# A mixture-of-experts stage rewritten as one program: router a sequence ahead, routed weights loaded in pieces, scratch cleared beside another stage

## The chip, the cores and the metric

The kernel runs on one core of a Trainium2 chip. The metric is the time of one execution on the device, in microseconds (us). The core has five engines that run their own instruction streams and meet at semaphores: TensorE (PE, matrix products), VectorE (DVE), ScalarE (ACT), GpSimd (POOL) and SyncE (SP, which here only starts transfers), and 16 DMA engines that move data between the chip's memory (HBM) and the core's own memory (SBUF). PE writes its results into banks of a small memory, PSUM, which DVE and ACT read.

## What is computed

16 sequences of 512 tokens with 256 features pass through six layers, each on the layer norm of x and with a residual sum. The two that the change is about are these (cut):

```python
def _L1_ffn_ref(x, router_w, router_b, routed_w1, routed_w3, routed_w2, shared_w1, shared_w3, shared_w2):
    logits = xf @ router_w + router_b                      # 8 experts
    topk_vals, topk_idx = jax.lax.top_k(logits, 2)
    sparse = sparse.at[jnp.arange(T)[:, None], topk_idx].set(topk_vals)
    gates = jax.nn.softmax(sparse, axis=-1)
    routed = jax.vmap(_expert, in_axes=(None, 0, 0, 0))(xf, routed_w1, routed_w3, routed_w2)
    routed_out = jnp.einsum('etd,te->td', routed, gates)
    shared_out = jax.vmap(_expert, in_axes=(None, 0, 0, 0))(xf, shared_w1, shared_w3, shared_w2).sum(axis=0)
    return (routed_out + shared_out).reshape(B, S, D)

def _expert(xf, w1, w3, w2):                    # hidden width 128
    return jax.nn.silu(xf @ w1) * (xf @ w3) @ w2

x = x + 0.5 * ffn(layernorm(x))
x = x + gated_linear_attention(layernorm(x))
x = x + 0.5 * ffn(layernorm(x))
x = x + 0.5 * moe(layernorm(x))        # moe0
x = x + attention(layernorm(x))        # 16 heads, softmax, a band of 0.1 near the diagonal
x = x + 0.5 * moe(layernorm(x))        # moe1, the same weights
```

## The kernel before

x (8192 tokens by 256 features, fp32) stays in SBUF for the whole kernel. The program is a row of stages with a barrier over all engines between them: constants, ffn0, `gla` (gated linear attention), ffn1, moe0, `att`, moe1. Within a stage each engine has a program written out by hand, in the order of the Python loops, and semaphores carry the dependences; no planner reorders anything. To keep fp32 precision every product is made of three PE products of parts: the high part of each operand (a rounded copy, usually made by ACT), and the low part (operand minus high, usually by DVE).

**The gated linear attention** (`gla_stage`) goes through the 16 sequences one by one. Per sequence a recurrence is solved by merging blocks in levels: PE makes 64 small products (L2201), DVE merges them (`merge`, L2514) and scales q (`raise_q`, L2530), POOL scales k (`raise_k`, L2453), and the next level's products wait for both. The DVE program also holds, for the sequence before, `o_norm` (reciprocal, then 4 instructions over 128x256, L2492) ahead of the level-1 merge, and the layer norm of the next sequence (4 instructions, L121).

**A MoE stage** (`moe_stage`) is five blocks one after another, each with a barrier behind it.

1. `prepare` loads the weights in 10 parts by SP (router, and w1, w3, w2 of experts 0 to 3, 4 to 7 and the two shared ones), makes the high parts on ACT (L637) and the low ones on DVE (L651). Attention uses the same helper with 4 parts. `whole_numbers` then makes tables of integers on POOL.
2. `dispatch_phase` goes through the 16 sequences. For sequence b DVE normalises the rows (L966), PE transposes them (L817), ACT copies the high part (L894) and DVE the low one (L972). PE computes the hidden layer of the first shared expert, with the router's products strewn between (`hidden`, L843, router L824 and L827), then the second expert, the transposes of b+1, the output (L858) and `places` (L868, L871, L873), which count the tokens ahead of each token per expert. DVE takes the logits (L994, L996), chooses the two best (`choose`, L1002 to L1021, ending with the margin that the gates come from), ACT makes the sigmoid of the margin (L914; sigmoid and silu need different tables of ACT, so a table load stands before each change), DVE writes gate and destination beside the row (L1027 to L1034) and the row index (L1039 to L1045). ACT makes the second copy of the rows (L900). POOL then issues 8 indirect DMAs (L946) that scatter the rows, 1040 bytes each, into an HBM scratch `expert_rows` by expert; a ring of 3 row buffers is freed by `sent`. `places` writes into the PSUM bank of the second shared expert, so it waits for that expert's silu.
3. `table_phase` computes on DVE, from the counts, which expert and which rows each of 39 tiles of 512 rows takes (L1110 to L1130).
4. `expert_phase`: ACT first issues 8 DMAs of 520 KB that zero the rows behind each expert's last (L1234), SP loads the tiles, and PE, ACT, DVE and POOL compute them and scatter the results.
5. `combine_phase` adds the two results of each token to x.

The lines of the dispatch loop of PE that matter, as written:

```python
for b in range(B):
    hidden(b, 0)
    if b:
        output(b - 1, 1)
    hidden(b, 1)
    if b + 1 < B:
        transpose(b + 1)
    output(b, 0)
    places(b)
```

## Time and profile before

| | us |
|---|---|
| time, median of 3 runs | 3865.52 |
| the runs | 3856.92, 3866.49, 3865.52 |
| the profiled execution, its time | 3864.73 |
| its span | 3862.7 |
| moe0: weights prepared | 1344.3 to 1361.2 |
| moe0: dispatch, first transposes to last row index | 1365.1 to 1605.6 |
| moe0: from there to the first tile's transposes | 1605.6 to 1636.8 |
| moe0: tiles | 1636.8 to 1913 |
| moe1: dispatch, the same bounds | 3238.8 to 3478.7 |
| gated linear attention | 408 to 1003 |

The span counts from the profiled execution's first instruction to its last; the time has 2 us around it. In the views below a time stamp is us from the span's start. A row of the timeline gives start, duration, engine, line, operation, output and input, how many like instructions are drawn together, and in square brackets how long the engine stood idle before it and who released it. In a row of a stretch, (x12) is how many instructions started there, PEclk is the clock that TensorE was granted as a share of the full one, and DMA the busy share of the 16 DMA engines.

### The profile page before, as it was taken

To read this page: it belongs to the slowest core of one execution; us is meant where nothing else is said; L and a number is where in the kernel's file an instruction comes from. 1 tells how busy PE (TensorE), PEld (TensorE's weight loads), DVE (VectorE), ACT (ScalarE), POOL (GpSimd) and SP (SyncE) were. 2 spreads that over 40 slices of the span, in tenths; PEclk is the share of its full clock that TensorE was granted. 3 is DMA by queue.
4 is the path that set the end of the run, shared out by engine and by line. 5 is a ranking of instruction groups with operands and counts; after the bars stand their busy time and mean duration, and the time that the engine had idled before them with its cause. 6 is when DMAs were issued, how large, how long until landed. Compare 5 with 4: busy or idle time off the path is not lost. (4 is left out here: it accounts for less than half of the span.)

```text
span 3862.7 us, 72003 instructions
## 1 busy us (share of the span) xinstructions
PE 3120.2 (81%) x24192; PEld 2382.7 (62%) x24192; DVE 2530.4 (66%) x5327; ACT 1824.5 (47%) x3241; POOL 1631.9 (42%) x1347
## 2 busy tenths in 40 slices
PE   5999688888799889688507999999999996995880
PEld 4888577777688778576404555555555554884660
DVE  5666577877566678555375777777777765774552
ACT  2444244444355445255303666666666664543550
POOL 1665222222366545456552333333333332553665
PEclk9999899999899989799857999999999997987995
DMA  3000000000000022355443324324233221224547
GB/s 110 0 0 0 16 0 0 0 0 0 1 0 0 19 77 74 105 161 158 149 143 101 93 70 114 82 78 111 74 88 100 74 66 64 77 74 156 158 151 281
DMA packets 204552, 292.07 MB, mean 76 GB/s; under 512 B 21472, under 2 KB 136560, under 8 KB 204416
## 3 DMA queue, kind: packets, MB, share of 16 engines
q1 hardware_dynamic: 149760, 189.51, 17.8%
q0 software_dynamic: 27264, 75.01, 5.1%
q10 hardware_dynamic: 27392, 25.83, 2.0%
q8 instruction: 74, 1.21, 0.1%
q14 instruction: 62, 0.51, 0.0%
HBM read 146.47 MB, written 143.28 MB: 75 GB/s over the span
## 5 line engine op out<-in xcount | busy, mean ns | idle before, releaser
L1945 DVE TENSOR_REDUCE neg_max_sb<-s_ps 128x1 f32<-128x512 f32 x1024 | 692.4, 687 | 292.4 <-PE s_ps L1672 271.6
L1835 ACT ACTIVATE prob_sb<-s_ps 128x512 f32<-128x512 f32 x1024 | 602.5, 600 | 393.6 <-PE s_ps L1684 384.3
L1592 POOL TENSOR_TENSOR prob_sb<-prob_sb,band_sb 128x520 f32<-128x520 f32 (+1 forms) x256 | 285.2, 1114 | 715.5 <-ACT prob_sb L1835 715.3
L529 POOL TENSOR_TENSOR f_sq_lo_sb<-f_sq_sb,f_sq_hi_sb 128x512 fp32r<-128x512 f32 x256 | 329.5, 1295 | 348.4 <-ACT f_sq_hi_sb L504 348.4
L1684 PE MATMUL s_ps<-q_stack_sb,k_stack_sb 128*128 128x512 f32 x1024 | 450.9, 441 | 8.0 <-ACT prob_sb L1835 7.5
L1672 PE MATMUL s_ps<-k_stack_sb,q_stack_sb 96*128 96x512 f32 x1024 | 425.9, 419 | 33.6 <-DMA k_stack_sb<-qk_scratch 23.3
L1280 POOL DMA_INDIRECT ranked_rows<-m_y_gated_sb,slot_dest_sb x312 | 328.0, 1051 | 263.5 <-ACT m_y_gated_sb L1261 177.5
L946 POOL DMA_INDIRECT expert_rows<-rows_sb,row_index_sb x256 | 258.0, 1008 | 245.3 <-DVE row_index_sb L1045 173.6
L1684 PEld LDWEIGHTS s_ps<-q_stack_sb,k_stack_sb 128*128 128x128 f32 x1024 | 193.2, 189 | 256.7 <-ACT prob_sb L1835 131.3
L499 ACT ACTIVATE f_relu_sb<-ffn_hp_ps 128x512 f32<-128x512 f32 x256 | 153.4, 599 | 314.6 <-PE ffn_hp_ps L452 314.0
L1705 PE MATMUL pv_ps<-prob_sb,v_ones_sb 128*32 128x512 f32 x2048 | 273.2, 606 | 0.9 <-POOL prob_sb L1592 0.9
L566 DVE TENSOR_TENSOR f_sq_sb<-ffn_hp_ps,f_relu_sb 128x512 f32<-128x512 f32 x256 | 174.6, 686 | 134.4 <-ACT f_relu_sb L499 99.4
L464 PE MATMUL ffn_y_ps<-w_proj_tern_sb,f_sq_lo_sb 128*128 128x256 f32 x1024 | 256.2, 283 | 0.0
L1672 PEld LDWEIGHTS s_ps<-k_stack_sb,q_stack_sb 96*128 96x128 f32 x1024 | 196.8, 192 | 96.0 <-DVE neg_max_sb L1945 50.3
L464 PE MATMUL ffn_y_ps<-w_proj_tern_sb,f_sq_hi_sb 128*128 128x256 f32 x1024 | 255.3, 282 | 0.7 <-POOL f_sq_lo_sb L529 0.7
L1196 PE MATMUL moe_b_h_ps<-xnT_hi_sb,tile_weights_sb 128*128 128x512 f32 x624 | 214.4, 425 | 43.9 <-issue 23.6
L1292 DVE TENSOR_TENSOR xnT_lo_sb<-moe_b_tp_ps,xnT_hi_sb 128x1024 fp32r<-128x1024 f32 x78 | 95.5, 1224 | 222.5 <-issue 112.4
L843 PE MATMUL moe_a_h_ps<-xnT_hi_sb,w_sb 128*128 128x512 f32 x512 | 212.2, 482 | 29.1 <-DVE xnT_lo_sb L972 24.7
L452 PE MATMUL ffn_hp_ps<-xnT_hi_sb,w_fc_hi_sb 128*128 128x512 f32 x512 | 210.6, 411 | 21.0 <-DVE xnT_lo_sb L158 19.8
L452 PE MATMUL ffn_hp_ps<-xnT_hi_sb,w_fc_lo_sb 128*128 128x512 f32 x512 | 203.8, 398 | 0.0
L464 PEld LDWEIGHTS ffn_y_ps<-w_proj_tern_sb,f_sq_hi_sb 128*128 128x128 f32 x1024 | 194.4, 190 | 11.9 <-POOL f_sq_lo_sb L529 1.1
L452 PE MATMUL ffn_hp_ps<-xnT_lo_sb,w_fc_hi_sb 128*128 128x512 f32 x512 | 201.7, 394 | 0.0
(346 smaller groups left out, 7936.9 us busy)
## 6 DMA issues: line engine op xcount, KB each, us to landing
expert_in_sb<-expert_rows SPq DMA_DIRECT2D x78, 520.0 KB
qk_scratch<-qk_hi_sb SPq DMA_DIRECT2D x128, 256.0 KB
q_stack_sb<-qk_scratch SPq DMA_DIRECT2D x128, 192.0 KB, 4.0
k_stack_sb<-qk_scratch SPq DMA_DIRECT2D x128, 192.0 KB, 4.2
token_results_sb<-ranked_rows SPq DMA_DIRECT2D x32, 512.0 KB, 6.3
token_results_sb<-ranked_rows ACTq DMA_DIRECT2D x32, 512.0 KB, 6.0
qk_scratch<-qk_lo_sb SPq DMA_DIRECT2D x64, 256.0 KB
expert_rows<-zero_rows_sb ACTq DMA_DIRECT2D x16, 520.0 KB, 5.6
```

What stands on the lines that cost most here:

```text
L452: op = nc.tensor.matmul(hp[j % 2][:, :], a[:, k, j * P:(j + 1) * P], x[:, k, :], start=(k == 0 and i == 0), stop=(k == KT - 1 and i == 2))
L464: op = nc.tensor.matmul(y[:, t, :], r[:, j, t * P:(t + 1) * P], w.proj[:, j, :], start=(j == 0 and t % 2 == 0 and i == 0), stop=(j == JT - ...
L529: nc.gpsimd.tensor_tensor(sql[:, j, :], sq[:, j % 2, :], as_f32(sqh[:, j, :]), ALU.subtract).then_inc(low_ready, 1)
L946: nc.gpsimd.indirect_dma_start(scratch.rows, bass.IndirectOffsetOnAxis(ap=idx[:, b % RB, r, t:t + 1], axis=0), rows[:, b % RB, r, t, :], N ...
L1196: op = nc.tensor.matmul(o[i % 2][:, :], wt[:, i % 2, part, k, :], x[:, k, :], start=(k == 0 and n == 0), stop=(k == KT - 1 and n == 2))
L1280: nc.gpsimd.indirect_dma_start(scratch.ranked, bass.IndirectOffsetOnAxis(ap=dst[:, i % META, t:t + 1], axis=0), ys[:, i % 2, t, :], None). ...
L1592: nc.gpsimd.tensor_tensor(pr, pr, bcast(band[:, off:off + hi - lo].unsqueeze(1), [P, GH, hi - lo]), ALU.mult).then_inc(band_done, 1)
L1672: nc.tensor.matmul(s1p[n % 2][:, :], qs[r, g // 2, u, qt * P:(qt + 1) * P], ks[r, g // 2, j, :], start=True, stop=True).then_inc(s1_ready, 1)
L1684: nc.tensor.matmul(s2p[i % 2][:, :], ks[:, g // 2, j, kt * P:(kt + 1) * P], qs[:, g // 2, u, :], start=True, stop=True).then_inc(s2_ready, 1)
L1705: op = nc.tensor.matmul(pvp[2 * HD * i:2 * HD * (i + 1), :], vaug[:, kt, GH * g + i, :], prob[:, kt % 2, i, :], start=(kt == 0), stop=(kt ...
L1835: nc.scalar.activation(prob[:, kt % 2, i, :], s2p[i % 2][:, :], ACT.Exp).then_inc(exp_done, 1)
L1945: nc.vector.tensor_reduce(nm[:, g % 2, 2 * (i % 2) + i // 2, qt:qt + 1], s1p[n % 2][:, :], AXIS_X, ALU.max, negate=True).then_inc(max_done, 1)
```

## The change

**The offset.** `prepare` computes once per stage, for all tokens, minus mean times rstd (`core.offset`, one more wait and one DVE instruction of 128x64). With it a normalisation is one ACT instruction, scale and bias by pointer.

**In the gated linear attention** the layer norm of the next sequence and `o_norm` move from DVE to ACT; DVE keeps two short instructions (`o_factors`). SP clears the whole scratch `expert_rows` (70144 rows of 1040 bytes, 72.9 MB) with 4 DMAs in this stage, from a zero tile, and the stage's end waits for them.

**In the MoE stages** `prepare` takes only the router and the shared experts (4 parts). The routed weights come in 12 pieces (two experts and one of w1, w3, w2 each, 128x512) inside the dispatch loop, in sequences 0 to 11: SP loads into a ring of 2, ACT copies the high part, POOL subtracts the low one. Dispatch, table and tiles are now one block. In the loop the layer norm of the rows moves from DVE to ACT, the second copy of the rows from ACT to POOL, and the router becomes 16 products by themselves, one sequence ahead of the shared experts. `places(b)` uses the same bank as before and so now waits for the silu of sequence b-1's second expert. The tails behind the experts' last rows are zeroed in their 4 payload columns alone (16 bytes a row), and SP waits for all 8 of these DMAs before the first tile. The tiles' own loops and the combining phase are computed as before.

The core of the diff, in the dispatch loop. TensorE:

```diff
-            for b in range(B):
-                hidden(b, 0)
-                if b:
-                    output(b - 1, 1)
-                hidden(b, 1)
-                if b + 1 < B:
-                    transpose(b + 1)
-                output(b, 0)
-                places(b)
-            output(B - 1, 1)
+                    for b in range(B + 1):
+                        if b < B:
+                            router(b)
+                        if b:
+                            hidden(b - 1, 0)
+                        if b >= 2:
+                            output(b - 2, 1)
+                        if b + 1 < B:
+                            transpose(b + 1)
+                        if b:
+                            hidden(b - 1, 1)
+                        if b < B:
+                            places(b)
...
+                        if b:
+                            output(b - 1, 0)
+                    output(B - 1, 1)
```

In `places`:

```diff
-                pe.wait_ge(silu_ready, 2 * b + 2)
+                        if b:
+                            pe.wait_ge(silu_ready, 2 * b)
```

ScalarE:

```diff
-            x_high(0)
-            second(0)
-            for b in range(B):
-                silu_of(b, 0)
-                high_of(b, 0)
-                silu_of(b, 1)
-                if b + 1 < B:
-                    x_high(b + 1)
-                share_of(b)
-                high_of(b, 1)
-                if b + 1 < B:
-                    second(b + 1)
+                    normalise(0)
+                    x_high(0)
+                    normalise(1)
+                    for b in range(B + 1):
+                        if b:
+                            silu_of(b - 1, 0)
+                            high_of(b - 1, 0)
+                        if b < B:
+                            share_of(b)
+                        if b + 1 < B:
+                            x_high(b + 1)
+                        if b < len(routed):
+                            weight_high(b)
+                        if b:
+                            silu_of(b - 1, 1)
+                        if b + 2 < B:
+                            normalise(b + 2)
+                        if b:
+                            high_of(b - 1, 1)
+                        if b == B - 1:
+                            act.wait_ge(table_ready, 1)
+                            for e in range(EXPERTS):
+                                row = act.value_load(tail[0:1, e:e + 1], min_val=0, max_val=EXPERTS * REGION - TOKENS)
+                                nc.scalar.dma_start(scratch.rows[bass.ds(row, TOKENS), DM:ROW]
+                                                    .rearrange("(t p) d -> p t d", p=P), zero[:, :, :]).then_inc(tail_zeroed, 16)
```

GpSimd:

```diff
+                    second(0)
+                    for b in range(B):
+                        if b < len(routed):
+                            weight_low(b)
+                        if b + 1 < B:
+                            second(b + 1)
+                        pool.wait_ge(second_ready, b + 1)
+                        pool.wait_ge(payload_ready, b + 1)
+                        pool.wait_ge(index_ready, b + 1)
```

VectorE:

```diff
+                    for b in range(B + 1):
+                        if b < B:
+                            take_logits(b)
+                            choose(b)
+                        if b:
+                            product(b - 1, 0)
+                            low_of(b - 1, 0)
+                        if b >= 2:
+                            update(b - 2)
+                        if b < B:
+                            payload(b)
+                        if b + 1 < B:
+                            x_low(b + 1)
+                        if b < B:
+                            index(b)
+                        if b == B - 1:
+                            table()
+                        if b:
+                            product(b - 1, 1)
+                            low_of(b - 1, 1)
```

SyncE, ahead of the first tile:

```diff
+                    sp.wait_ge(table_ready, 1)
+                    for i in range(RB):
+                        sp.wait_ge(sent[i], PER_SENT * ((B - 1 - i) // RB + 1))
+                    sp.wait_ge(tail_zeroed, 16 * EXPERTS)
```

In the gated linear attention, on ScalarE, VectorE and SyncE in turn:

```diff
+                def o_norm(b):
+                    act.wait_ge(o_off, b + 1)
+                    for t in range(NC):
+                        op = nc.scalar.activation(og[:, t, :], og[:, t, :], ACT.Identity, bias=off[:, t:t + 1],
+                                                  scale=ors[:, t:t + 1])
+                    op.then_inc(on_ready, 1)
...
                     merge(b, 0)
                     if before:
-                        o_norm(b - 1)
+                        o_factors(b - 1)
                     merge(b, 1)
...
                     raise_q(b, 4)
-                    if more:
-                        norm.normalise(dve, b + 1)
                     merge(b, 5)
...
+                for i in range(CLEAR):
+                    part = slice(left * i // CLEAR, left * (i + 1) // CLEAR)
+                    sp.dma_start(cleared[:, part, :], bcast(zeros[:, :].unsqueeze(1), [P, part.stop - part.start, TILES * ROW])
+                                 ).then_inc(clear_done[i], 16)
```

ACT's instructions in the dispatch loop, one sequence's turn from a silu on, before (m_silu_sb is the silu, m_act_hi_sb the high part of the hidden layer, xnT_hi_sb that of the transposed rows):

```order
L904 ACTIVATE m_silu_sb<-moe_a_h_ps 128x512
L894 CAST xnT_hi_sb<-moe_a_tp_ps 128x1024
L914 ACT_TABLE_LOAD
L914 ACTIVATE share_sb<-margin_sb 128x32
L910 CAST m_act_hi_sb<-m_act_sb 128x512
L900 COPY rows_sb<-rows_sb 128x4x256
L904 ACT_TABLE_LOAD
L904 ACTIVATE m_silu_sb<-moe_a_h_ps 128x512
```

and with the change, in the same loop of ACT (xn_sb is where the silu now goes, w_sb a routed weight's high part):

```order
L1008 ACTIVATE xn_sb<-moe_h_ps 128x512
L1014 CAST m_act_hi_sb<-m_act_sb 128x512
L1018 ACT_TABLE_LOAD
L1018 ACTIVATE share_sb<-margin_sb 128x32
L1004 CAST xnT_hi_sb<-moe_tp_ps 128x1024
L1023 CAST w_sb<-routed_values_sb 128x512
L1008 ACT_TABLE_LOAD
L1008 ACTIVATE xn_sb<-moe_h_ps 128x512
L996 ACTIVATE rows_sb<-x_resident_sb,ln_minus_mean_rstd_sb,ln_rstd_sb 128x256 x4
```

Both silus of a sequence stood between two sigmoids with no table load between them; now the sigmoid of the next sequence stands between them, and the second silu, for which `places` waits, comes behind the sigmoid, the transposed rows' copy, the weight's copy and a table load.

PE's instructions around `places` before, with the next sequence's hidden layer and router behind it:

```order
L858 MATMUL moe_a_y_ps<-w2h_sb,m_act_lo_sb 128x256
L868 MATMUL moe_a_h_ps<-chosen_sb,below_sb 128x32
L871 MATMUL moe_a_h_ps<-chosen_sb,ones_sb 128x24
L871 MATMUL moe_a_h_ps<-chosen_sb,ones_sb 128x16
L871 MATMUL moe_a_h_ps<-chosen_sb,ones_sb 128x8
L873 MATMUL moe_a_h_ps<-seen_sb,ones_sb 128x32
L843 MATMUL moe_a_h_ps<-xnT_hi_sb,w_sb 128x512
L827 MATMUL moe_a_tp_ps<-router_w_hi_lo_sb,xnT_hi_sb 128x16
L843 MATMUL moe_a_h_ps<-xnT_hi_sb,w_sb 128x512
L824 MATMUL moe_a_tp_ps<-router_w_hi_lo_sb,xnT_lo_sb 128x8
```

and with the change, around `places` on PE:

```order
L883 MATMUL moe_h_ps<-xnT_hi_sb,w_sb 128x512 x2
L883 MATMUL moe_h_ps<-xnT_lo_sb,w_sb 128x512
L904 MATMUL moe_h_ps<-chosen_sb,below_sb 128x32
L907 MATMUL moe_h_ps<-chosen_sb,ones_sb 128x24
L907 MATMUL moe_h_ps<-chosen_sb,ones_sb 128x16
L907 MATMUL moe_h_ps<-chosen_sb,ones_sb 128x8
L909 MATMUL moe_h_ps<-seen_sb,ones_sb 128x32
L893 MATMUL moe_y_ps<-w2h_sb,m_act_hi_sb 128x256
```

`places` now stands directly behind the second expert's hidden layer (L883), whose silu it waits for, and an output (12 products, L893) stands behind it. Behind that output come the router's products of the next sequence, 16 of them without anything between, and then the hidden layer:

```order
L871 MATMUL moe_tp_ps<-router_w_hi_lo_sb,tile_weights_sb 128x8
L869 MATMUL moe_tp_ps<-router_w_hi_lo_sb,xnT_hi_sb 128x16
L871 MATMUL moe_tp_ps<-router_w_hi_lo_sb,tile_weights_sb 128x8
L883 MATMUL moe_h_ps<-xnT_hi_sb,w_sb 128x512 x2
L883 MATMUL moe_h_ps<-xnT_lo_sb,w_sb 128x512
```

(tile_weights_sb serves there as the third buffer of the transposed rows' low part.) Before, these 16 stood one or two at a time behind the twelve products of L843.

## Rows read from the trace of the kernel before

**Rows 1.** The page, part 1: busy us, share of the span, instructions of each engine

```profile
PE 3120.2 (81%) x24192; PEld 2382.7 (62%) x24192; DVE 2530.4 (66%) x5327; ACT 1824.5 (47%) x3241; POOL 1631.9 (42%) x1347
```

**Rows 2.** Stretches: gated linear attention, then moe0's weights, dispatch, dispatch to tiles

```profile
core 0: us, PE busy (x) PEld busy (x) DVE busy (x) ACT busy (x) POOL busy (x), PEclk, DMA share, GB/s
408.00:1003.00 595.00, 474.18 (x9344) 413.73 (x9344) 444.20 (x925) 235.64 (x388) 135.98 (x114) 0.97 0.00 1
1344.30:1361.20 16.90, 0.00 (x0) 0.00 (x0) 9.88 (x11) 8.50 (x11) 0.03 (x1) 0.50 0.76 234
1365.10:1605.60 240.50, 223.41 (x1306) 200.12 (x1307) 176.79 (x552) 115.13 (x144) 120.98 (x120) 0.88 0.19 69
1605.60:1636.80 31.20, 2.09 (x11) 1.73 (x9) 6.43 (x23) 0.00 (x0) 7.77 (x8) 0.50 0.39 128
```

**Rows 3.** The same view: moe1's dispatch

```profile
3238.80:3478.70 239.90, 223.35 (x1306) 200.16 (x1307) 176.35 (x551) 115.12 (x144) 121.48 (x120) 0.88 0.20 69
```

**Rows 4.** Timeline of one sequence in the gated linear attention, DVE, POOL and PE

```profile
645.54 2.58 DVE L2492 TENSOR_SCALAR g_og_sb<-g_og_sb,g_mv_sb,g_rstd_sb 128x256 f32<-128x256 f32 x4
646.36 1.61 POOL L2453 TENSOR_TENSOR g_ks_sb<-g_ks_sb,g_f_sb 128x512 f32<-128x512 f32 x1 [15.81 <-PE g_h_ps L2201]
649.18 0.53 PE L2201 MATMUL g_h_ps<-g_qp_sb,g_ks_sb 128*32 128x32 f32 x37 [1.41 <-DVE g_qp_sb L2530]
...
657.66 1.37 DVE L121 TENSOR_SCALAR xn_sb<-x_resident_sb,ln_mean_var_sb,ln_rstd_sb 128x256 f32 x4
```

**Rows 5.** The view by stretches: attention's weights, 4 parts

```profile
1995.90:2003.50 7.60, 0.00 (x0) 0.00 (x0) 3.29 (x5) 4.11 (x6) 0.02 (x1) 0.50 0.48 139
```

**Rows 6.** The same view: two sequences of moe0's dispatch, one after the other

```profile
1420.80:1434.00 13.20, 12.38 (x83) 11.15 (x82) 11.17 (x36) 7.20 (x9) 7.96 (x9) 1.00 0.23 81
1434.00:1451.90 17.90, 17.07 (x83) 15.31 (x82) 11.32 (x36) 7.19 (x9) 11.51 (x12) 0.71 0.24 87
```

**Rows 7.** Timeline of moe0's dispatch, PE from one output to the next

```profile
1479.59 0.36 PE L858 MATMUL moe_a_y_ps<-w2h_sb,m_act_hi_sb 128*128 128x256 f32 x1
...
1481.09 0.32 PE L868 MATMUL moe_a_h_ps<-chosen_sb,below_sb 128*128 128x32 f32 x2
...
1483.12 0.50 PE L843 MATMUL moe_a_h_ps<-xnT_hi_sb,w_sb 128*128 128x512 f32 x1 [0.82 <-DVE xnT_lo_sb L972]
...
1487.69 0.36 PE L858 MATMUL moe_a_y_ps<-w2h_sb,m_act_hi_sb 128*128 128x256 f32 x1
```

**Rows 8.** Timeline of the same stretch, DVE: choose, then a product

```profile
1478.58 0.42 DVE L1002 TENSOR_TENSOR above_sb<-logits_sb 128x256 f32<-128x256 f32 x1
...
1481.74 0.19 DVE L1021 SCALAR_TENSOR_TENSOR margin_sb<-logits_sb,both_sb 128x32 f32<-128x32 f32 x1
...
1482.98 0.68 DVE L978 TENSOR_TENSOR m_act_sb<-moe_a_h_ps,m_silu_sb 128x512 f32<-128x512 f32 x1
```

**Rows 9.** Timeline of the same stretch, ACT

```profile
1479.87 1.01 ACT L894 CAST xnT_hi_sb<-moe_a_tp_ps 128x1024 fp32r<-128x1024 f32 x1 [1.67 <-PE moe_a_tp_ps L817]
1480.91 1.28 ACT L914 ACT_TABLE_LOAD   x1
1482.20 0.23 ACT L914 ACTIVATE share_sb<-margin_sb 128x32 f32<-128x32 f32 x1
1483.70 0.62 ACT L910 CAST m_act_hi_sb<-m_act_sb 128x512 fp32r<-128x512 f32 x1 [1.27 <-issue]
...
1486.58 0.60 ACT L904 ACTIVATE m_silu_sb<-moe_a_h_ps 128x512 f32<-128x512 f32 x1
```

**Rows 10.** Groups by line: busy us, mean ns of one | idle time before them

```profile
L946 POOL DMA_INDIRECT expert_rows<-rows_sb,row_index_sb x256 | 258.0, 1008 | 245.3 <-DVE row_index_sb L1045 173.6 <-issue 71.7
```

**Rows 11.** Timeline from moe0's dispatch to its tiles, DVE, ACT's queue, PE

```profile
1620.92 0.17 DVE L1110 COPY count_sb<-moe_t_ps_ps 128x8 f32<-128x8 f32 x1 [12.34 <-PE moe_t_ps_ps L1098]
...
1626.80 12.62 ACTq L1234 DMA_DIRECT2D expert_rows<-zero_rows_sb  x8
...
1636.80 1.12 PE L1189 MATMUL moe_b_tp_ps<-identity_sb,expert_in_sb 128*128 128x128 f32 x4 [15.92 <-DMA expert_in_sb<-expert_rows]
```

1067 lines of the change are left out of this document (517 added, 550 removed).

## The prediction

> **What bounds the kernel now.** The page's first part comes first: PE is busy 81% of the span, DVE 66%, ACT 47%, POOL 42% [rows 1]. That is an average over unlike stages, so the view by stretches comes next, cut at the places that the change touches [rows 2]. In the gated linear attention (595 us) PE is busy 474 and DVE 444, and the DMA engines do nothing. While moe0's weights are prepared PE does nothing for 16.9 us; the transfers run at 234 GB/s and DVE and ACT work only as parts arrive. In the dispatch PE is busy 223 of 240.5 us, at a mean clock of 0.88. Between the last row index and the first tile lie 31.2 us in which PE does nearly nothing. moe1's dispatch is the same within 0.6 us [rows 3], so every term of a MoE stage counts twice.
>
> So in the dispatch PE is the bound, and what matters there is the clock. Two sequences, one after the other, with the same instructions take 13.2 us at clock 1.00 and 17.9 us at 0.71 [rows 6]: a fall to 1.2 GHz costs 4.7 us. 0.71 over 17.9 us is 10.4 us at half speed. A mean of 0.88 over 240.5 us [rows 2] is 58 us at half speed; some 16 of these are its start (the stretch before it stands at 0.50, and PE keeps that until large products have run), and the other 42 are four falls of 10.4. PE's rows show what they follow: an output, then places, 10 small products in 1.21 us (1481.09 to 1482.30), and a wait of 0.82 us for the low part of the next rows [rows 7]. That is 2.0 us without a large product, in every sequence; four of 16 such stretches end in a fall.
>
> **The change, part by part.** The sum is made against the profiled execution, 3864.7 us, which lies 0.8 under the median of the three runs.
>
> *Gated linear attention.* o_norm holds DVE for 2.58 us from 645.54. Only then can DVE merge level 1 and scale q, and PE waits 1.41 us for it, until 649.18; POOL's k is ready at 647.97 (646.36 + 1.61) [rows 4]. Without o_norm POOL ends last: PE starts some 0.95 us sooner. The layer norm (1.37 us of DVE [rows 4]) goes too, in a place where DVE is not always last; I take 0.3 of it. With 15 such sequences that is 15 x 1.25, about -18. Bounds: 15 x (1.41 + 0.5) = -29, and +5 if ACT, which gets 8 instructions of under 0.60 each (that is what 512 columns take [rows 9]), hands its next copy over late; ACT is busy only 236 of 595 us [rows 2]. The clearing of 72.9 MB takes 312 us at the 234 GB/s of the weight loads, under 595 us in which nothing else uses DMA [rows 2]: nothing. Should it not fit, only the end of the stage would wait, by the time over 595.
>
> *Prepare.* Attention's four parts are ready in 7.6 us [rows 5]; the MoE stage's ten take 16.9 [rows 2]. Four parts here too: -9.3 each. The extra DVE instruction hides under the loads.
>
> *Dispatch, start.* At half speed the transposes take 1.6 and the router's products 3.6; with the high part 1.0, the low part 1.2, logits and choose 3.8, places 1.8 and index 1.0 that is 14 us from the first transposes to the first index (an estimate from the prices below).
>
> *Dispatch, per sequence.* By work PE would need the 12.4 us that it is busy now [rows 6]. But places(b) now waits for silu(b-1,1), and that stands at the end of a chain that begins with the router's last product: two short additions 0.4 (like the 0.19 of L1021), choose 3.35 (1478.58 to 1481.93), product 0.68 [rows 8], high part 0.62, table load 1.28, sigmoid 0.23, copy of the rows' high part 1.01, the weight's high part 0.62 (same shape as L910), table load 1.28, silu 0.60 [rows 9]: 10.1, with hand-overs 10.2 us. ACT's table loads come in its stream behind the instruction ahead, and a load does not wait for its sigmoid's input (1480.91, before the margin at 1481.93 [rows 8, 9]); but the load stands behind the high part, which waits for the product, so nothing hides it now. In these 10.2 us PE has two hidden layers, one output and the transposes: 12 products of 512 columns at 2.4 GHz are 2.56 us, 2.8 with their starts, one output is 1.5 (1479.59 to 1481.09 [rows 7]), and the transposes are what is left of the 12.4 after hidden and router, hidden, two outputs and places: 12.4 - 4.57 - 2.8 - 3.0 - 1.2 = 0.8. So 2 x 2.8 + 1.5 + 0.8 = 7.9. PE then stands idle for some 2.3 us ahead of places in every sequence. Behind the silu follow places 1.2, output 1.45 and the router's 16 products: hidden and router together take 4.57 (1483.12 to 1487.69 [rows 7]), so 1.8. Period: 10.2 + 1.2 + 1.45 + 1.8 = 14.65 us, and 14.05 in the three last, which have no weight to copy. The layer norm on ACT (4 instructions) lies behind the silu and so beside places, output and router. At full clock: 14 + 12 x 14.65 + 3 x 14.05 = 232 us, against 240.5: -8.5.
>
> The Trainium skill, "ScalarE: Activation LUTs" (What ACT_TABLE_LOAD costs), puts a change of table at about 2.66 us, with a drain behind the load. The row shows 1.29 from the start of the load to its sigmoid; by the page's figure a sequence would be 2.8 us longer and the kernel some 80 us slower, and the trace speaks against it.
>
> *Dispatch, clock.* Now the stretch without a large product is 2.3 + 1.2 = 3.5 us, then 1.45 us of output, then 1.8 us of router products of 16 and 8 columns: 6.75 us with one output in it, where before there were 2.0. A longer sparse stretch cannot make fewer falls than now unless it is its idle part alone that counts, so I take a fall in every second sequence, 8 of 16, at 4.7 each: 38 us. Bounds: none and 15. The dispatch takes 270, +29.5 each.
>
> *POOL.* 8 indirect DMAs take 10.3: 1.01 each, and 0.3 of issue ahead of each but the first (71.7 us over 224 [rows 10]). The weight's low part is 128x512 with two inputs, 1.61 [rows 4]; the second copy, 128x1024, costs between nothing and twice that. At 2.0, POOL needs 13.9 a sequence, under 14.65: nothing. At 3.2 it would be 15.1 and bind by 0.5.
>
> *Gap to the tiles.* Now: index, 8 indirect DMAs, barrier, table from 1620.92, then ACT issues 8 tail DMAs in 12.62 us from 1626.80, and a tile's rows come at 1636.80 [rows 11]. With the change the table (5 us with its count) starts behind the index and beside POOL; one product and one high part later, at about 6.5, ACT starts to issue: 6.5 + 12.6 = 19. SP waits for all eight, then loads: from the first tail's issue to the transposes are 10.0 us today, less its own issue of 1.6, so 8.4 for a landing and a load, and 8 to 9.5 with the last one's short runs. Transposes at 27 to 28.5, against 31.2 now: -2.7 each, between -6 (a landing of 16-byte runs is quick) and +3 (if such runs take 6 us more than full rows). The shared experts of the last sequence (two hidden layers, two outputs) fill part of it. Tiles and combining are untouched: nothing.
>
> Sum: -18 + 2 x (-9.3 + 29.5 - 2.7) = -18 + 35 = +17: 3881.7, say **3882 us**. A measurement of this kernel can tell about 0.3%, 12 us, from no change.
>
> **The rivals.**
>
> *The falls stay at four or so in a dispatch* (3 to 5), because they depend on how the sequences' period meets the chip's, not on the stretch's length. For: only 4 of 16 equal stretches fell. Then 4 x 4.7 = 19, dispatch 251, +10.5 each: -18 + 2 x (-9.3 + 10.5 - 2.7) = -21, 3844 us.
>
> *No falls, faster.* PE never stands idle for long: 2.3 us at a stretch. Then dispatch is 232: -18 + 2 x (-9.3 - 8.5 - 2.7) = -59, 3806 us. Against it: falls came after waits of 0.82 us [rows 7]. The Trainium skill, "TensorE: Matmul & The Clock Gate" (Why this matters for your kernels), warns of idle gaps of PE between bursts longer than these; by that rule nothing here would fall, and by it nothing should have fallen before either, which the clock of 0.71 contradicts.
>
> *A fall in every sequence, slower still.* 15 x 4.7 = 70, dispatch 302: -18 + 2 x (-12 + 62) = +82, 3947 us. For: no stretch of PE's from the silu's wait to the hidden layer is without its sparse 3.5 us.
>
> *The chain is hidden.* The change does what its order says, router one sequence ahead, only if choose and the sigmoid lie beside PE's work. If the chain were under 7.9 us, PE would be the bound again at 12.4 and four falls, 14 + 15 x 12.4 + 19 = 219: -18 + 2 x (-9.3 - 21.5 - 2.7) = -85, 3780. It would take 2.3 us out of ACT's and DVE's rows, and nothing in the profile offers them.
>
> *POOL binds.* With the copy at 3.2 and its two-input work slowed beside DVE by 1 us, the period is 16: +1.3 x 15 x 2 = +40 on top, 3921.
>
> **How the numbers follow.** Half the falls (6 to 10): 0.42. Four or so: 0.20. None to two: 0.13. Over ten falls: 0.10. Chain hidden: 0.02. POOL or the new waits in the gap or in the linear attention cost 20 to 60 more: 0.13. The forecast's own range is 3860 to 3905. Below the forecast lie 3844 and 3806, above 3921 and 3947; 8 in 10 are held from 3806 to 3925. Faster by over 0.3% (under 3853): most of four falls, and fewer: 0.31. Within 0.3%: the low end of the forecast and the high end of four falls: 0.19. Slower: 0.50.
>
> **What would show it.** In the profile after: PE waits some 2.3 us ahead of places (L904) for ACT's silu (L1008) in each sequence, and the row indexes (DVE's last instruction of a sequence) come 14.65 us apart at full clock. Dispatch at a mean clock of about 0.82. Prepare 7.6 us. PE's wait at the linear attention's level 1 falls from 1.41 to about 0.5, released by POOL. DMA in that stage about 120 GB/s over its length. The forecast is wrong if the clock in the dispatch is 0.88 or more, if the period differs from 14.65 by over 0.5, or if the linear attention does not shorten.

## The result and the profile after

| | before | after |
|---|---|---|
| time, median (4 runs each, on one chip) | 3861.22 us | 3975.48 us |
| the runs | 3849.82 to 3866.49 | 3972.56 to 3980.58 |
| profiled execution's span | 3862.7 | 3970.8 |

The change makes the kernel slower: ratio 1.0301, 95% interval 1.0273 to 1.033. The forecast was 3882, with a range of its own of 3860 to 3905; the direction was right, the size was not. By stages, from the two profiles (first to last instruction, or between the marks of the forecast):

| us | before | after | forecast of the difference | measured |
|---|---|---|---|---|
| gated linear attention | 594.3 | 601.9 | -18 | +7.6 |
| moe0, weights prepared | 16.9 | 6.8 | -9.3 | -10.1 |
| moe0, dispatch | 240.5 | 309.3 | +29.5 | +68.8 |
| moe1, dispatch | 239.9 | 310.3 | +29.5 | +70.4 |
| moe0, last index to first tile | 31.2 | 25.3 | -2.7 | -5.9 |
| moe1, last index to first tile | 31.8 | 25.7 | -2.7 | -6.1 |

moe1's preparation loses 10 us too, the tiles take 1 to 2 us less a stage, and the other stages differ by no more than 4. Together these are the 108 us between the spans.

The stretches of the changed kernel that answer to [rows 2, 3], in the same view: linear attention, moe0's weights, dispatch, dispatch to tiles, and moe1's dispatch.

```profile
413.10:1015.00 601.90, 481.77 (x9344) 420.65 (x9344) 405.95 (x817) 297.14 (x512) 136.26 (x115) 0.95 0.31 122
1352.50:1359.30 6.80, 0.00 (x0) 0.00 (x0) 3.03 (x6) 2.40 (x5) 0.00 (x0) 0.50 0.41 118
1363.10:1672.40 309.30, 250.39 (x1248) 224.05 (x1249) 156.53 (x481) 131.11 (x195) 149.47 (x148) 0.77 0.18 62
1672.40:1697.70 25.30, 14.59 (x70) 12.70 (x69) 9.89 (x28) 2.95 (x5) 7.80 (x8) 0.80 0.39 102
...
3283.10:3593.40 310.30, 259.80 (x1248) 230.94 (x1249) 155.68 (x481) 130.77 (x195) 149.84 (x148) 0.74 0.18 62
```

VectorE is 38 us less busy in the linear attention and ScalarE 61 more, and the stage is longer all the same, with the DMA engines at a share of 0.31. In the dispatch TensorE is busier than before (250 against 223 us) with 58 fewer products starting in it, because its clock is 0.77 against 0.88. It is idle for 59 us, where before it was for 17.

The row indexes of moe0 come 16.8 to 21.4 us apart, seven of the 15 steps between 20.2 and 20.7 (before: 13.2, or 17.9 with a fall). The same view over four stretches in a row:

```profile
1413.90:1424.10 10.20, 10.20 (x41) 9.51 (x41) 5.14 (x17) 2.29 (x5) 5.99 (x6) 0.50 0.26 88
1424.10:1434.40 10.30, 6.94 (x44) 5.86 (x42) 4.96 (x14) 6.32 (x10) 4.20 (x5) 1.00 0.14 45
1434.40:1444.60 10.20, 10.20 (x41) 9.52 (x41) 5.13 (x17) 2.26 (x5) 5.96 (x6) 0.50 0.25 87
1444.60:1454.80 10.20, 6.80 (x43) 5.75 (x42) 4.97 (x15) 6.21 (x10) 4.24 (x5) 1.00 0.12 43
```

In this part the clock is at 1.2 GHz half the time, in stretches of 10.2 us, and a period is one such stretch and one at full clock.

What TensorE waits for in the dispatch, from the view of waits (us in all, times, longest):

```profile
PE moe_h_ps L904 <- issue: 54.4, 15, 5.6
...
DVE place_sb L1215 <- PE moe_h_ps L909: 43.0, 15, 3.6
...
ACT m_act_hi_sb L1014 <- PE moe_y_ps L893: 38.1, 10, 4.4
```

The first row is the wait ahead of places for the silu. A wait in this view holds the time in which the producer still works as well. In the second row that is nearly all of it: places' semaphore rises within 0.01 us of its last product's end in all 16 sequences. In the third it is not, as the next rows show.

One sequence of it in the timeline, VectorE's product, TensorE's last output product and places, and ScalarE's chain:

```profile
1425.36 0.69 DVE L1153 TENSOR_TENSOR m_act_sb<-moe_h_ps,xn_sb 128x512 f32<-128x512 f32 x1 [0.71 <-PE moe_h_ps L883]
...
1426.39 0.28 PE L893 MATMUL moe_y_ps<-w2h_sb,m_act_lo_sb 128*128 128x256 f32 x1
...
1433.68 0.38 PE L904 MATMUL moe_h_ps<-chosen_sb,below_sb 128*128 128x32 f32 x2 [3.36 <-issue]
...
1428.09 0.62 ACT L1014 CAST m_act_hi_sb<-m_act_sb 128x512 fp32r<-128x512 f32 x1 [3.93 <-PE moe_y_ps L893]
1428.73 1.28 ACT L1018 ACT_TABLE_LOAD   x1
1430.02 0.23 ACT L1018 ACTIVATE share_sb<-margin_sb 128x32 f32<-128x32 f32 x1
1430.16 0.99 ACT L1004 CAST xnT_hi_sb<-moe_tp_ps 128x1024 fp32r<-128x1024 f32 x1
1431.05 0.62 ACT L1023 CAST w_sb<-routed_values_sb 128x512 fp32r<-128x512 f32 x1
1431.69 1.28 ACT L1008 ACT_TABLE_LOAD   x1
1432.98 0.60 ACT L1008 ACTIVATE xn_sb<-moe_h_ps 128x512 f32<-128x512 f32 x1
```

ScalarE's part is the one that the forecast listed, with its durations. But the chain has a hole at its head: the product ends at 1426.05, and the high part starts at 1428.09. It waits for the previous sequence's output as well, and that output's last product ends at 1426.67 by the record. For 1.4 us more nothing happens on ScalarE. The trace also records when a semaphore rises, and this one rises at 1428.01. Such a hole stands in the kernel before as well, in a stage that the forecast did not look into, the tiles. Here the last product of an output and the gating that waits for it:

```profile
1744.36 0.28 PE L1206 MATMUL moe_b_y_ps<-w2h_sb,m_act_lo_sb 128*128 x1
...
1748.31 1.57 ACT L1261 ACTIVATE m_y_gated_sb<-moe_b_y_ps,slot_gate_sb 128x256 f32<-128x256 f32 x4 [2.46 <-remote]
```

The product is done at 1744.64, and ScalarE, idle for 2.46 us, goes on at 1748.31, 3.67 us later. "Remote" means that the profile did not find who ended the wait; the record has the product's semaphore rise at 1748.29.

### The profile page after: what moved, and what is told of

Read it like the earlier page. It is cut to its first block and busy times, and to the rows that moved or that the text cites. A ratio compares the mean times of both kernels' runs of the same rounds, so it can differ in the third digit from the quotient of the medians.

```text
span 3970.8 us, 71995 instructions
## 1 busy us (share of the span) xinstructions
PE 3214.5 (81%) x24192; PEld 2464.9 (62%) x24192; DVE 2446.2 (62%) x5079; ACT 1914.4 (48%) x3475; POOL 1679.1 (42%) x1404
## 5 line engine op out<-in xcount | busy, mean ns | idle before, releaser
L1130 POOL DMA_INDIRECT ranked_rows<-rows_sb,slot_dest_sb x312 | 320.5, 1027 | 256.1 <-ACT rows_sb L1075 172.0
L952 PE MATMUL moe_h_ps<-xnT_hi_sb,tile_weights_sb 128*128 128x512 f32 x624 | 214.1, 425 | 38.6 <-issue 29.3
L1280 DVE TENSOR_TENSOR xnT_lo_sb<-moe_tp_ps,xnT_hi_sb 128x1024 fp32r<-128x1024 f32 x78 | 95.5, 1224 | 198.0 <-ACT xnT_hi_sb L1055 169.5
L883 PE MATMUL moe_h_ps<-xnT_hi_sb,w_sb 128*128 128x512 f32 x512 | 202.4, 483 | 0.0
L465 PEld LDWEIGHTS ffn_y_ps<-w_proj_tern_sb,f_sq_lo_sb 128*128 128x128 f32 x1024 | 195.7, 191 | 9.9
```

Source lines behind the costliest of these rows:

```text
L465: op = nc.tensor.matmul(y[:, t, :], r[:, j, t * P:(t + 1) * P], w.proj[:, j, :], start=(j == 0 and t % 2 == 0 and i == 0), stop=(j == JT - ...
L952: op = nc.tensor.matmul(o[i % 2][:, :], wt[:, i % 2, part, k, :], x[:, k, :], start=(k == 0 and n == 0), stop=(k == KT - 1 and n == 2))
L1130: nc.gpsimd.indirect_dma_start(scratch.ranked, bass.IndirectOffsetOnAxis(ap=dst[:, i % META, t:t + 1], axis=0), ys[:, i % 2, t, :], None). ...
```

## The experiments

Every time stands beside runs of the kernel before on the same chip; dispatch is moe0's unless said. All edits are to the changed kernel, if no other is named. Theory A is the forecast's: idle time of TensorE ahead of places, with small products behind it, makes the clock fall. Dispatch times are of the profiled execution. In the four runs with one or four indirect DMAs most rows never reach the tiles, so their times say nothing of a usable kernel.

**silu_first.** ScalarE's second silu goes ahead of the sigmoid:

```diff
+                        if b:
+                            silu_of(b - 1, 1)
                         if b < B:
                             share_of(b)
...
                             weight_high(b)
-                        if b:
-                            silu_of(b - 1, 1)
```

> The changed kernel with one move on ScalarE: the silu of sequence b-1's second expert goes ahead of the sigmoid, the rows' copy and the weight's copy. In the changed kernel the dispatch takes 309 us in both stages, one row index every 20 us, with TensorE idle 3.4 us ahead of places and a fall to 1.2 GHz in every sequence. Theory A (that idle time together with the small products behind it makes the fall, and the silu's place makes the idle time): the idle time ahead of places goes under 0.5 us, few or no falls, period 13.0 us, dispatch 205 to 222, kernel 3976 - 2 x 95 = 3790 (3770 to 3815). Theory B (the router's 16 small products standing by themselves make the falls): falls stay in most sequences, dispatch 270 or more, kernel 3900 or more.

Measured: 3897.55 us, ratio 1.0097 (1.0076 to 1.0118); dispatch

```profile
1359.80:1626.70 266.90, 232.46 (x1264) 202.73 (x1265) 165.66 (x482) 129.91 (x194) 151.03 (x148) 0.83 0.21 72
```

266.9 us, 42 less than the change, so the silu's place costs that much. But the periods are 15.3 us at full clock, not 13.0, and 18.2 with a fall, and falls stay in most sequences. Theory A's figures are missed by far, theory B's by 3 us; that the router's products alone don't make falls is shown further down, by order_b_one_scatter and one_scatter_fill10, where they stand as here and the clock doesn't fall behind the start. Something else lengthens the sequence.

**fill10.** Ten large products more, ahead of places:

```diff
+                        if 0 < b < B:
+                            pe.wait_ge(silu_ready, 2 * b - 1)
+                            for i in range(10):
+                                nc.tensor.matmul(h1[0][:, :], w13[:, 0, KT * EXPERTS, :], xh[(b - 1) % XB][:, 0, :],
+                                                 start=True, stop=True)
                         if b < B:
                             places(b)
```

> The changed kernel with 10 more products of 128x512 on TensorE, 2.35 us at full clock, ahead of places, into the bank of the first expert's hidden layer that nobody reads then; their results are overwritten. Theory A (the falls come from the idle time, and cost some 5 us each): no idle time worth the name ahead of places at full clock, falls in few sequences, although TensorE has more work: period 14.7 to 15.6, dispatch 235 to 255, kernel 3976 - 2 x 64 = 3850 (3835 to 3880). Theory C (the falls cost nothing, the chain over ScalarE sets the period at either clock): dispatch 309 and more, kernel 3976 to 4020.

Measured: 3946.93 us, ratio 1.0223 (1.0203 to 1.0243); dispatch

```profile
1358.50:1653.00 294.50, 257.21 (x1407) 226.90 (x1407) 156.23 (x482) 131.50 (x195) 149.06 (x148) 0.87 0.19 66
```

294.5 us at clock 0.87. TensorE is given 150 more large products and the stage gets 15 us shorter: the falls do cost time. But eight falls stay, and the period is 18.0 us even from 1389.3 to 1407.3, at a clock of 0.99, far over the 14.65 of the chain as forecast. Theory A explains 15 us here, not 60. What fills this sequence, TensorE's last product of an output and ScalarE:

```profile
1395.76 0.28 PE L893 MATMUL moe_y_ps<-w2h_sb,m_act_lo_sb 128*128 128x256 f32 x1
...
1397.51 0.62 ACT L1019 CAST m_act_hi_sb<-m_act_sb 128x512 fp32r<-128x512 f32 x1 [3.65 <-PE moe_y_ps L893]
...
1401.77 1.01 ACT L1009 CAST xnT_hi_sb<-moe_tp_ps 128x1024 fp32r<-128x1024 f32 x1 [2.10 <-remote]
```

The product was done at 1396.16, the output's semaphore rises at 1397.43: a hole of 1.35 us. The transposes behind that output end at 1396.9 by the record, their semaphore rises at 1401.75, and ScalarE stands idle for 2.10 us. Together 3.45 us, what lies between 18.0 and the 14.5 that one_scatter_fill10 shows below.

**high_own_wait.** The first expert's high part waits for the output that reads its own buffer:

```diff
-                        if e == 1:
-                            op.then_inc(y_ready, 1)
+                        op.then_inc(y_ready if e == 1 else y0_ready, 1)
...
                         if b:
-                            act.wait_ge(y_ready, b)
+                            act.wait_ge(y_ready if e == 1 else y0_ready, b)
```

> The changed kernel, but the high part of the first expert's hidden layer waits for the output that last read its own buffer, not for both outputs of the sequence before (one semaphore more). In the changed kernel this copy starts 2.0 us after its product, since the output in front of it is late. Theory D (this wait is part of the chain to the silu and a good share of the loss): idle time ahead of places down from 3.4 to some 2.3 us, full-clock period 15.6 to 14.5, fewer falls, dispatch 255 to 285, kernel 3976 - 2 x 40 = 3896 (3875 to 3930). Theory A alone (any idle time of over 2 us there brings the fall): a fall in every sequence still, dispatch 290 to 305, kernel 3940 to 3970.

Measured: 3942.82 us, ratio 1.0213 (1.0189 to 1.0237); dispatch

```profile
1362.80:1655.70 292.90, 243.58 (x1248) 216.95 (x1249) 159.92 (x481) 131.72 (x195) 149.81 (x148) 0.78 0.19 66
```

292.9 us, one index every 19.0 us: 16 us from one wait that looked free. It is part of the loss; the falls stay (theory A's 290 to 305).

**order_b.** New orders on ScalarE and VectorE:

```diff
                             high_of(b - 1, 0)
+                        if b:
+                            silu_of(b - 1, 1)
+                        if b + 1 < B:
+                            x_high(b + 1)
                         if b < B:
                             share_of(b)
-                        if b + 1 < B:
-                            x_high(b + 1)
                         if b < len(routed):
                             weight_high(b)
                         if b:
-                            silu_of(b - 1, 1)
+                            high_of(b - 1, 1)
                         if b + 2 < B:
                             normalise(b + 2)
-                        if b:
-                            high_of(b - 1, 1)
...
-                        if b < B:
-                            payload(b)
                         if b + 1 < B:
                             x_low(b + 1)
                         if b < B:
                             index(b)
+                        if b:
+                            product(b - 1, 1)
+                        if b < B:
+                            payload(b)
                         if b == B - 1:
                             table()
                         if b:
-                            product(b - 1, 1)
                             low_of(b - 1, 1)
```

> The changed kernel with new orders on ScalarE and VectorE and nothing else: ScalarE silu 0, high 0, silu 1, rows' copy, sigmoid, weight's copy, high 1, layer norm; VectorE rows' low part, index and second product ahead of the payload. By the durations in the trace TensorE then has no idle time ahead of places and the period is its own work, 12.4 to 12.6 us; no falls: dispatch 195 to 205, against 309, kernel 3976 - 2 x 109 = 3758 (3745 to 3790), under the kernel before (3861). If the scatter on GpSimd binds (10.3 + 1.3 + 1.0 and hand-overs), period 13.0 to 13.5: 3775 to 3790. If the router's small products alone bring falls (theory B), dispatch 240 or more and kernel 3840 or more.

Measured: 3838.85 us, ratio 0.9946 (0.9927 to 0.9965), already under the kernel before; dispatch

```profile
1362.00:1595.40 233.40, 208.23 (x1244) 181.94 (x1245) 176.13 (x478) 128.95 (x194) 149.41 (x145) 0.92 0.24 80
```

233.4 us with an index every 15.2, not 12.5. Its timeline says what is in the way. TensorE's last product of places, VectorE's two first instructions of the index, GpSimd's subtraction and copy:

```profile
1461.39 0.39 PE L909 MATMUL moe_h_ps<-seen_sb,ones_sb 128*128 128x32 f32 x2
...
1465.16 0.19 DVE L1215 TENSOR_TENSOR place_sb<-moe_h_ps,moe_whole_sb 128x32 f32<-128x32 f32 x1 [2.07 <-remote]
1465.39 2.31 DVE L1218 TENSOR_TENSOR mask_product_sb<-rank_mask_sb,place_sb 128x64 f32<-128x64 f32 x1
...
1465.32 1.31 POOL L1110 TENSOR_TENSOR w_sb<-routed_values_sb,w_sb 128x512 fp32r<-128x512 f32 x1
1466.55 1.05 POOL L1104 COPY rows_sb<-rows_sb 128x1024 f32<-128x1024 f32 x1
```

places' last product is done at 1461.78; VectorE, which has been idle for 2.07 us, sees it at 1465.16. The bank was not ready late: TensorE had gone on with an output at 1462.11. The semaphore is 3.4 us late by its record too. Then the multiplication over 128x64, 0.22 us elsewhere, takes 2.31 and ends 0.1 behind GpSimd's copy. The Trainium skill, "GPSIMD Engine Reference" (Specifications), says that VectorE and GpSimd share their way into SBUF and get into each other's way when VectorE's instruction has two SBUF inputs; this one has two, and these rows agree.

In the kernel before such late semaphores of TensorE stand in two stages: in the linear attention, the feed-forward stages and attention there is none among some 3000, in the tiles they come in about half of the cases, and in the dispatch places' is 3.3 to 3.8 us late in 11 of 16 sequences. Those two are the stages in which GpSimd issues indirect DMAs. That is theory E.

**after_one_scatter.** One indirect DMA a sequence instead of 8. Left out are 7 of 8 scatters to the scratch; so that nothing undefined is read, all tiles' results go to spare rows and the result scratch is cleared too:

```diff
-            PER_SENT = 16 * TOP_K * TILES
+            PER_SENT = 16
...
-                        for r in range(TOP_K):
-                            for t in range(TILES):
+                        for r in range(1):
+                            for t in range(1):
```

> The changed kernel with one of the 8 indirect DMAs of a sequence on GpSimd, the other seven left out (so most rows never reach the scratch; the tiles' results all go to the spare rows, which needs a clearing of the result scratch beside the linear attention too). In the trace of the changed kernel the semaphore of an output's last product reaches ScalarE 1.2 to 1.8 us after the product's recorded start where 0.3 is usual; such late semaphores of TensorE stand in the dispatch and tile stages alone, the two with indirect DMAs. Theory E (the indirect DMAs make TensorE's semaphores late): all of them at 0.3 to 0.5 us now, high part 1.3 us sooner, dispatch 265 to 285 instead of 309. Theory F (they are late for a reason of TensorE's own): the same 1.2 to 1.8 us, dispatch 300 to 310.

Measured: 3893.53 us against 3868.37 (two executions), ratio 1.0072 (1.0045 to 1.0099); dispatch

```profile
1365.00:1639.50 274.50, 238.19 (x1248) 211.04 (x1248) 158.96 (x481) 130.82 (x195) 46.13 (x43) 0.80 0.06 19
```

274.5 us, 35 less. The output's last product and the high part that waits for it:

```profile
1460.66 0.28 PE L893 MATMUL moe_y_ps<-w2h_sb,m_act_lo_sb 128*128 128x256 f32 x1
...
1461.03 0.62 ACT L1014 CAST m_act_hi_sb<-m_act_sb 128x512 fp32r<-128x512 f32 x1 [3.75 <-PE moe_y_ps L893]
```

Done at 1460.94, gone on with at 1461.03. Every semaphore of TensorE in this dispatch comes 0.3 to 0.65 us after its product's start. Periods are 14.5 us without a fall and 17.6 to 20.2 with most of the falls. Theory E holds, F falls. DMA traffic as such and GpSimd's own time are no rivals here: in the changed kernel's dispatch no engine's wait of note is ended by a DMA, and VectorE's index takes its usual 0.22 us beside GpSimd.

**order_b_one_scatter.** The same omission in order_b.

> The same omission in the reordered kernel (order_b: dispatch 233.5, period 15.2 against the 12.5 that its work needs). There the semaphore of places comes 3.6 us after its last product's start, and the index's multiplication on VectorE takes 2.2 us where 0.22 is usual, beside GpSimd's subtraction and copy. Theory E: places' semaphore at 0.3 to 0.4, the index 3 us sooner, GpSimd's two element-wise instructions no longer beside it, period 12.4 to 12.8, dispatch 198 to 207. Theory F: period 14.5 to 15.2, dispatch 225 to 234.

Measured: 3743.52 us against 3868.37; dispatch

```profile
1363.70:1560.50 196.80, 192.73 (x1248) 175.12 (x1249) 167.83 (x477) 129.82 (x194) 46.54 (x43) 0.95 0.09 27
```

196.8 us, just under theory E's 198 to 207, an index every 12.2, no fall behind the start. The 36 us between 233.4 and 196.8 are what the indirect DMAs cost order_b: late semaphores, and GpSimd's two instructions beside the index. This run does not part the two.

**four_scatters.** Four of 8 (one rank's rows):

```diff
-            PER_SENT = 16 * TOP_K * TILES
+            PER_SENT = 16 * TILES
...
-                        for r in range(TOP_K):
+                        for r in range(1):
```

> The changed kernel with 4 of the 8 indirect DMAs of a sequence (the second rows' left out), otherwise as after_one_scatter. Its four are over 5 us after the index, before the next sequence's choose has ended. If a semaphore of TensorE is late only while an indirect DMA is being issued or is under way, the output's semaphore (8 to 12 us after the index) comes at 0.3 us as with one, and places' and the router's too: dispatch 272 to 285. If the number of indirect DMAs in the program counts and not their place in time, it is 0.7 us or more late in most sequences: dispatch 290 to 305.

Measured: 3895.81 us against 3862.07 (three executions), ratio 1.008 (1.0056 to 1.0104); dispatch

```profile
1364.70:1635.90 271.20, 234.20 (x1244) 207.62 (x1245) 158.98 (x481) 130.98 (x195) 90.29 (x88) 0.81 0.13 42
```

271.2 us, about the same as with one, and all semaphores on time. So it is not that such DMAs are in the program. Nor is it enough that one is being issued, as the expectation had it: the router's semaphores fall between the first issue and 1.3 us behind the start of the fourth in all 15 sequences, and are on time.

The records of the changed kernel, both dispatches, say more. These are the semaphores of router, transposes, outputs and places by where their last product ends among the eight indirect DMAs of a sequence, late meaning over 0.3 us behind that end (of the hidden layers' some records are missing):

| product ends | semaphores | late |
|---|---|---|
| while the first four are issued | 28 | 0 |
| from the fifth's issue to 2 us behind the eighth's start | 44 | 40, by 0.5 to 5.0 us |
| later | 42 | 0 |

So the lateness begins with the fifth of a run of indirect DMAs, and with four there is none. Why with the fifth, no run tells. Routers' semaphores (27 of the 28) and places' (29 of the 42) are on time in the changed kernel; late are those of the outputs and the transposes.

**one_scatter_fill10.** after_one_scatter and fill10 together.

> The changed kernel with one indirect DMA a sequence instead of 8 (as in after_one_scatter) and with the 10 products ahead of places (as in fill10). Filling alone took the dispatch from 309 to 295 us, the omission alone to 274, where the periods are 14.5 us without a fall and 17.6 to 20.2 with one. Theory A, in what is left of it (with semaphores on time the falls are what lengthens the sequences over the chain's 14.5): no falls, every period 14.6 to 15.2, dispatch 233 to 245. Theory I (filling saves only what it happens to save, the falls come all the same): dispatch 265 to 280.

Measured: 3821.47 us against 3862.07 (two executions); dispatch

```profile
1362.10:1597.80 235.70, 229.66 (x1398) 202.96 (x1399) 158.06 (x481) 131.02 (x195) 46.55 (x43) 0.95 0.07 23
```

235.7 us at clock 0.95, no fall behind the start, and every period 14.5 to 15.1 but the first (16.2) and the last (13.6). With this the four cells are full (moe0's dispatch, us; moe1 in brackets):

| | 8 indirect DMAs | 1 |
|---|---|---|
| nothing ahead of places | 309.3 (310.3) | 274.5 (273.4) |
| ten products ahead of places | 294.5 (298) | 235.7 (235.5) |

The two causes don't add up: seven indirect DMAs cost 35 us with the waits as they are and 59 with the waits filled, and filling brings 15 us beside eight of them and 39 beside one.

**no_pieces.** The routed weights back in the preparing block:

```diff
-                + weight_parts("shared", EXPERTS, E))
+                + weight_parts("routed", 0, 4) + weight_parts("routed", 4, 8) + weight_parts("shared", EXPERTS, E))
-        routed = [part for e in range(0, EXPERTS, 2) for part in weight_parts("routed", e, e + 2)]
+        routed = []
```

> The changed kernel with the routed weights back in the preparing block (10 parts there, none in the dispatch loop: no copy on ScalarE, no subtraction on GpSimd, no loads by SyncE beside it). Preparing 16.9 us instead of 6.8, so +10 a stage. In the dispatch the chain to the second silu is 0.62 us shorter in 12 sequences; if each sequence still holds a fall, -8 to -20 (309 to 290 to 301) and the kernel 3955 to 3980; if the shorter idle time lets every second fall go, dispatch 270 to 285, kernel 3925 to 3945.

Measured: 3974.03 us, ratio 1.0276 (1.0259 to 1.0294), where the change has 1.0301 (1.0273 to 1.033); preparing and dispatch

```profile
1356.10:1372.90 16.80, 0.00 (x0) 0.00 (x0) 10.11 (x12) 8.55 (x11) 0.00 (x0) 0.50 0.76 235
1376.60:1675.60 299.00, 248.91 (x1248) 222.24 (x1249) 156.69 (x481) 124.72 (x183) 135.05 (x136) 0.77 0.15 54
```

The pieces save 10 us ahead of the dispatch and cost 10 in it here (moe1: 15), where ScalarE's copy lies in the chain. Whether they are a gain in an order where it doesn't, no run tests.

**clear_only.** The kernel before with the clearing of the scratch:

```diff
+                sp.wait_ge(zeroed, 3)
+                for i in range(CLEAR):
+                    part = slice(left * i // CLEAR, left * (i + 1) // CLEAR)
+                    sp.dma_start(cleared[:, part, :], bcast(zeros[:, :].unsqueeze(1), [P, part.stop - part.start, TILES * ROW])
+                                 ).then_inc(clear_done[i], 16)
```

> The kernel before, with the clearing of the whole scratch in the gated linear attention as its only change (the full-row zeroing of the tails stays). In the changed kernel that stage is 7.5 us longer than before although its steady sequence is 0.57 us shorter; its first three sequences, with the DMA engines at share 1.02, take 13 us more. Theory G (the clearing traffic holds up the first sequences, whose instructions are being fetched then): linear attention +10 to +17 us, kernel 3858 + 13 = 3871 (3866 to 3876). Theory H (the moves to ScalarE cost it): no difference, 3858.

Measured: 3876.79 us against 3868.37, ratio 1.0026 (1.0017 to 1.0036); the stage

```profile
413.20:1023.80 610.60, 481.43 (x9344) 419.48 (x9344) 445.76 (x929) 234.17 (x384) 137.50 (x115) 0.95 0.30 120
```

610.6 us against 594.3, +16.3, as theory G has it; the steady sequence is 35.13 us in both, so all of it lies in the first ones. (The kernel's time grows by 8 us only; stages that the edit doesn't touch differ by some us from one execution profiled to the other.) In the first sequences all computing engines stand idle at the same time, three times for 1.5 to 2.5 us and once for 2.9, which happens neither in the kernel before nor in clear_late. The first time ends with TensorE:

```profile
435.45 0.44 PE L2214 MATMUL g_h_ps<-g_qp_sb,g_ks_sb 128*32 128x32 f32 x16 [2.61 <-issue]
```

**gla_moves_only.** The kernel before with layer norm and o_norm on ScalarE, as in the change.

> The kernel before, with layer norm and o_norm of the linear attention moved to ScalarE as its only change (with the offset that this needs), no clearing. By the steady sequence of the changed kernel (34.56 against 35.13 us): 15 x 0.57 = -8.5 us, kernel 3858 - 8 = 3850 (3845 to 3855), within what a measurement can tell. Theory H: the first sequences take 10 us or more longer here too, kernel 3860 or more.

Measured: 3848.14 us against 3868.37, ratio 0.996 (0.9944 to 0.9975); the stage

```profile
413.30:997.90 584.60, 472.56 (x9344) 413.26 (x9344) 405.27 (x817) 297.12 (x512) 134.47 (x114) 0.97 0.00 1
```

-9.7 us there; the rest of the 20 us lies in stages that the edit doesn't touch.

**clear_late.** One wait more ahead of the clearing:

```diff
                 sp.wait_ge(zeroed, 3)
+                sp.wait_ge(x_done, 2)
```

> The changed kernel, but SyncE starts the clearing of the scratch only when sequence 1 of the linear attention is done, when every engine has been through its loop's code once. Clearing alone cost the kernel before 16 us of that stage (610.6 against 594.3), the moves alone gave back 10. If the clearing's traffic costs only while code is fetched (theory G): linear attention 585 to 590 us instead of 602, kernel 3976 - 14 = 3962 (3957 to 3968). If it costs wherever it lies: 600 and more, kernel 3974 to 3980.

Measured: 3960.61 us, ratio 1.0234 (1.0216 to 1.0253); the stage

```profile
413.40:999.90 586.50, 474.91 (x9344) 415.35 (x9344) 405.05 (x817) 297.15 (x512) 135.35 (x115) 0.97 0.32 125
```

586.5 us, 15.4 less than the change, with the same bytes moved. The clearing costs 2 us here and 16 at the stage's start.

**order_c.** order_b, with the index last on VectorE:

```diff
-                        if b < B:
-                            index(b)
                         if b:
                             product(b - 1, 1)
                         if b < B:
                             payload(b)
+                        if b:
+                            low_of(b - 1, 1)
+                        if b < B:
+                            index(b)
                         if b == B - 1:
                             table()
-                        if b:
-                            low_of(b - 1, 1)
```

> order_b with one more move on VectorE: the index of sequence b goes last, behind the second product, the payload and the second low part, so that nothing stands behind the wait for places' semaphore, which comes 3.6 us late in order_b (theory E, shown by the runs with one indirect DMA: there it comes at 0.3 us and the dispatch takes 197 us against 233.5). If what the late semaphore costs is only what queues behind it: period 15.2 down to 12.5 to 13.2, dispatch 203 to 214, kernel 3839 - 2 x 25 = 3789 (3775 to 3805). If the late semaphores of the router and of the outputs still bind: period 14 to 15, kernel 3810 to 3835.

Measured: 3797.28 us, ratio 0.9825 (0.9811 to 0.984); dispatch

```profile
1357.90:1571.10 213.20, 201.74 (x1256) 178.07 (x1257) 180.98 (x483) 130.48 (x195) 150.73 (x147) 0.94 0.26 89
```

213.2 us, an index every 13.3, both in or next to the forecast of the first case. places' semaphore is on time in eight of 16 sequences here and 0.4 to 4.4 us late in the others, the router's 2 us late in most; VectorE waits for places only twice, 2.7 us in all. The conversion that ends the index, 128x8 with one input, takes 2.5 us here instead of 0.17, and ends with GpSimd's copy.

**order_c_late_tails.** order_c, high_own_wait and clear_late together, and half of the tail DMAs on SyncE's queue:

```diff
-                            for e in range(EXPERTS):
+                            for e in range(EXPERTS // 2):
                                 row = act.value_load
...
+                    for e in range(EXPERTS // 2, EXPERTS):
+                        row = sp.value_load(tail[0:1, e:e + 1], min_val=0, max_val=EXPERTS * REGION - TOKENS)
+                        sp.dma_start(scratch.rows[bass.ds(row, TOKENS), DM:ROW]
+                                     .rearrange("(t p) d -> p t d", p=P), zero[:, :, :]).then_inc(tail_zeroed, 16)
```

> Everything that the runs point to, together: order_c, the clearing started after sequence 1 of the linear attention, the high part with a wait for its own output only, and the 8 tail DMAs split between ScalarE's and SyncE's queues (in the changed kernel ScalarE issues all eight in 12 us, and SyncE waits for them before the first tile). Against order_c: -14 for the clearing, 0 to -4 for the wait, -5 a stage for the tails: kernel 3789 - 26 = 3763 (3745 to 3785), against 3861 of the kernel before.

Measured: 3773.51 us, ratio 0.9761 (0.9749 to 0.9774) against 3867.18, faster than both kernels. One of its six runs took 12474 us, which nothing here explains; the others lie between 3766.73 and 3780.70. Linear attention, dispatch, dispatch to tiles:

```profile
413.50:1000.00 586.50, 475.85 (x9344) 415.56 (x9344) 404.91 (x817) 297.28 (x512) 135.53 (x115) 0.97 0.32 125
1347.60:1566.20 218.60, 206.38 (x1259) 181.78 (x1260) 172.71 (x484) 130.75 (x195) 150.52 (x146) 0.92 0.25 86
1566.20:1590.50 24.30, 10.51 (x57) 9.21 (x56) 9.30 (x28) 3.62 (x5) 10.50 (x11) 0.72 0.42 109
```

The time is within the forecast. The tails' split brings the gap from order_c's 30.1 to 24.3. moe0's dispatch is 5 us longer than in order_c and moe1's 4 shorter, so that high_own_wait's edit brings anything on top of order_c is not shown.

## Why the forecast was wrong, step by step

**The chain: right at full clock.** The forecast put the period without a fall at 14.65 us, the wait ahead of places at 2.3, the dispatch at full clock at 232. With semaphores on time and the wait filled, the periods are 14.5 and the dispatch 235.7; after_one_scatter shows the wait at 1.5 to 2.8 us, nine of 15 at 2.0 to 2.2. The start was 15.2 us to the first index (14 forecast). The order of ScalarE as the source is shown by silu_first. In a sequence with a fall the high part also waits 0.7 to 1.1 us for the output of the sequence before, with semaphores on time too; the forecast didn't have that.

**The clock: near where the semaphores are on time.** There the falls cost 274.5 - 235.7 = 39 us, in nine stretches at half speed behind the start; the forecast had eight and 38. "Every second sequence" was a choice between none and 15, so that the count fits is partly luck. As built there are 12 such stretches and 143 us at half speed in all, against 112 in after_one_scatter: the late semaphores leave TensorE idle for longer, 3.36 us ahead of places in the sequence shown, 5.6 at most. The rival "a fall in every sequence" was nearest in what happens, and it said 302 us. By the rule on idle gaps of the Trainium skill, "TensorE: Matmul & The Clock Gate" (Why this matters for your kernels), nothing should fall in after_one_scatter, whose waits there are at most 2.8 us; the trace speaks against it again.

**The step that failed: "high part 0.62" right behind "product 0.68", and the copy of the rows' high part with no wait of its own.** The forecast took a semaphore to rise when the product's record ends, and put the term at nothing. In the changed kernel the output's semaphore, for which the high part waits, rises 0.2 to 3.3 us behind that end in moe0, and the transposes' up to 5.0. Between product and high part ScalarE stands 26.5 us in moe0's 14 sequences, against 7.7 in after_one_scatter, and it waits 4.9 us for the transposes, against none: 24 of the 35 us by which the two dispatches differ. The other 11 go with the 31 us more at half speed, which is argued and not shown by a run of its own. places' semaphore is not part of it: late in the kernel before and in order_b, it is on time in all 32 sequences of the changed kernel. In the kernel before its lateness costs the dispatch nothing that shows: places ends at 1482.30, and VectorE has other work until 1485.70, when it first looks.

The term is 309.3 - 274.5 = 35 us in moe0 and 37 in moe1, where one indirect DMA gives 273.4 us against 310.3. That is 72 us of the 91 between the forecast's difference, +17, and that of the spans, +108. The evidence was in the trace before: an idle time of 2.46 us in the tiles that ended in "remote", and tiles whose gating waited though the product was done. Of the forecast's three signs of being wrong two came, a period far from 14.65 and a linear attention that did not shorten; the clock of 0.77 was not one.

**The second step that failed: the clearing, put at "nothing".** It cost 16.3 us (clear_only), all at the stage's start. The first sequences of the change, in the view by stretches:

```profile
416.00:456.00 40.00, 26.68 (x497) 21.58 (x495) 14.08 (x22) 11.20 (x17) 6.12 (x5) 0.71 1.02 406
456.00:497.00 41.00, 32.41 (x554) 28.12 (x548) 22.94 (x41) 18.62 (x33) 8.76 (x7) 0.81 1.03 405
497.00:534.00 37.00, 30.58 (x589) 26.78 (x590) 25.99 (x52) 18.72 (x34) 9.30 (x7) 0.95 1.03 407
534.00:568.50 34.50, 28.91 (x594) 25.33 (x590) 25.26 (x52) 18.52 (x33) 8.28 (x7) 1.00 1.03 407
```

The first four sequences end at 456, 497, 534 and 568.5: 43 us from the stage's start, then 41.0, 37.0 and 34.5, though the DMA engines are as busy in the fourth (1.03) as in the third. In the kernel before they end at 449.1, 485.4, 520.8 and 555.9: 36.3, 36.3, 35.4 and 35.1. Sequence 0 is written out and the others are a loop, so engines go through code for the first time only here, and code comes by DMA too: the queues that the page names "instruction" have their packets in this stage up to 504.0 and none in the 200 us behind. With the clearing they come 9 us apart (432.2, 441.4, 450.2, 458.9), without it 4 to 6 (429.0, 433.3, 438.5, 444.5 in gla_moves_only). And while the first three of those come, all computing engines stand idle together, from 432.3 to 434.4, 441.0 to 443.7 and 450.3 to 452.5. Started behind that, the clearing costs 2 us (clear_late). That engines wait for code is what these rows fit; no run isolates it. What the forecast missed is that bandwidth was free, but the first passes were not independent of it.

**The moves to ScalarE** bring 9.7 us, not 18: 35.13 to 34.53 us a sequence. The forecast had taken 0.95 for o_norm and 0.3 for the layer norm; together they gave 0.60. The size of the first term was wrong. Level 1 in the changed kernel, GpSimd, VectorE and TensorE:

```profile
658.20 1.51 POOL L2484 TENSOR_TENSOR g_ks_sb<-g_ks_sb,g_f_sb 128x512 f32<-128x512 f32 x1 [15.79 <-PE g_h_ps L2210]
...
658.62 1.64 DVE L2558 TENSOR_TENSOR g_qp_sb<-g_qp_sb,g_f_sb 128x512 f32<-128x512 f32 x1
...
660.39 0.76 PE L2210 MATMUL g_h_ps<-g_qp_sb,g_ks_sb 128*32 128x32 f32 x64 [0.78 <-DVE g_qp_sb L2558]
```

TensorE waits 0.78 us instead of 1.41, and not the 0.5 of the forecast, and VectorE ends the wait, not GpSimd. Without o_norm VectorE's scaling of q now runs beside GpSimd's of k, and it takes 1.64 us where it took 0.68 behind it. The 0.63 won there are all of the 0.60; the layer norm's move gave nothing that shows.

**Prepare** -10.1 (forecast -9.3), and **POOL** as forecast: its copy of 128x1024 takes 1.03 us, the subtraction 1.26, and it does not bind. **The gap** came to -6 instead of -2.7, since ScalarE issues the eight tail DMAs in 9.5 us (1679.03 to 1688.55), not 12.6. Its start, 6.6 us behind the last index, and the 9.2 us from the last issue to the first tile are as forecast (6.5, and 8 to 9.5). **The table loads** cost 1.28 us each (1428.73 to 1430.02), as in the rows of before.

**The sum again.** Of +17 the measured terms make +108: the late semaphores 72, the linear attention 26 (+7.6 instead of -18), the rest of both dispatches 8 (the start 1.2 each, the falls 1 each, the chain the rest), prepare -2, the gaps -7, and -6 in stages that the change does not touch or hardly touches.

## What to carry to other kernels

Before a chain is hung on a semaphore, read from the trace when its waiters go on, not when the producer ends; if no waiter is idle there, the lateness is unseen and not absent. In an engine's hand-written order put what waits for a late event last, and what another engine waits for first: new orders on two engines, with no instruction removed, were worth 96 us in moe0's dispatch (309.3 to 213.2) and 94 in moe1's. When work is taken off one engine, see what its next instruction will then run beside: two engines' work in SBUF at the same time took longer here than one behind the other. A long transfer beside a stage cost 16 us when it began with the stage, and 2 when it began behind the stage's first pass through its code.

## What the runs showed of the hardware

- A semaphore that TensorE raises came 0.3 to 0.65 us after the start of the product that raises it where one or four indirect DMAs a sequence were issued (all of moe0's dispatch). Beside eight it did so too for products that end while the first four are issued (28 of 28); from the fifth's issue to 2 us behind the eighth's start 40 of 44 rose 0.5 to 5.0 us behind the product's end.
- The lateness does not hold TensorE itself: in order_b its next output started at 1462.11, 3 us before VectorE saw places' end.
- Beside two element-wise instructions of GpSimd a multiplication of VectorE with two SBUF inputs, 128x64, took 2.31 us instead of 0.22 (order_b), and a conversion of 128x8 with one input 2.5 instead of 0.17 (order_c). Beside one of GpSimd a multiplication of 128x512 took 1.64 instead of 0.68.
- While HBM was being cleared at 406 GB/s, the packets of the instruction queues came 9 us apart instead of 4 to 6, and all computing engines stood idle for 2.1 to 2.7 us at three of them.
- Clearing HBM from one zero tile in SBUF ran at 405 to 407 GB/s; the weight loads run at 234.
- With one indirect DMA a sequence TensorE's clock fell nine times in 15 sequences with waits of 1.5 to 2.8 us and ten small products behind large ones, and not once when ten large products filled the wait. Beside eight indirect DMAs it still fell eight times with the ten products.
